# Slot stage of a mixture of experts: marks of the second list two token tiles at a time, inputs turned three slots ahead

## The reference

```python
x = x + attention(layernorm(x), ctx, ...)
y = layernorm(x)
router_weights = softmax(y @ W_router.T + b_router)          # 8 per token
topk_w, topk_idx = top_k(router_weights, 2)                  # the best 2 are kept
x = x + sum over the 2 kept e of topk_w * (y @ W_experts[e].T + b_experts[e])
```

## Time and profile before

| what | value |
|---|---|
| median of 3 runs | 2568.51 us (2566.49 to 2568.64) |
| profiled execution: time | 2569.43 us |
| profiled execution: span | 2567.6 us |
| PE busy | 2446.4 us (95% of the span) |
| DVE busy | 2155.9 us (84%) |
| ACT busy | 1854.7 us (72%) |
| POOL busy | 426.9 us (17%) |

### The profile page before, as it was taken

One profiled execution on the slowest core, in us unless ns is written; L12 is line 12 of the kernel. 1 busy time (PEld: TensorE's weight loads), 2 busy tenths in 40 slices (PEclk: granted clock), 3 DMA queues, 4 the chain that ended last, 5 costly groups with the idle time before them and its releaser, 6 DMA issues. The chain is left out here.

```text
span 2567.6 us, 37487 instructions
## 1 busy us (share of the span) xinstructions
PE 2446.4 (95%) x13675; PEld 1318.7 (51%) x13675; DVE 2155.9 (84%) x1895; ACT 1854.7 (72%) x2174; POOL 426.9 (17%) x522
## 2 busy tenths in 40 slices
PE   8999579999999999999999999999999969879998
PEld 7878324444444444444444444444444438768786
DVE  4368479999999999999999999999999956666565
ACT  3123369999998999999999989999999835513343
POOL 2123200000000000000000000000000024325664
PEclk9999789999999999999999999999999989969999
DMA  7435781111152111124111112311111058624473
GB/s 266 157 137 208 173 213 26 26 29 27 26 124 51 26 30 26 29 56 116 26 30 26 40 33 64 94 26 26 47 26 26 18 170 294 215 84 135 127 235 119
DMA packets 141949, 231.62 MB, mean 90 GB/s; under 512 B 25027, under 2 KB 70595, under 8 KB 141005
## 3 DMA queue, kind: packets, MB, share of 16 engines
q1 hardware_dynamic: 119532, 177.58, 24.2%
q0 software_dynamic: 22240, 51.68, 6.7%
HBM read 155.33 MB, written 91.66 MB: 96 GB/s over the span
## 5 line engine op out<-in xcount | busy, mean ns | idle before, releaser
L1050 ACT ACTIVATE probs<-psum 128x1024 f32<-128x1024 f32 x1600 | 1513.2, 1035 | 137.7 <-PE psum L1204 130.7
L1204 PE MATMUL psum<-q_st,k_st 97*128 97x512 f32 x3200 | 923.0, 419 | 43.3 <-DMA q_st<-shift_scratch 23.8
L1204 PEld LDWEIGHTS psum<-q_st,k_st 97*128 97x128 f32 x3200 | 549.3, 189 | 618.3 <-ACT probs L1050 412.3
L1112 DVE TENSOR_TENSOR even_sums<-even_sums,probs 128x2048 f32<-128x2048 f32 x352 | 806.5, 2291 | 18.3 <-ACT probs L1050 18.3
L1225 PE MATMUL psum<-probs,v_st 128*32 128x512 f32 x6400 | 800.4, 601 | 0.0
L1112 DVE TENSOR_TENSOR odd_sums<-odd_sums,probs 128x2048 f32<-128x2048 f32 x320 | 732.1, 2288 | 1.0
L1225 PEld LDWEIGHTS psum<-probs,v_st 128*32 128x32 f32 x6400 | 152.3, 108 | 353.1 <-issue 273.2
L1922 PE MATMUL psum<-we_hi,wo 128*128 x624 | 218.7, 412 | 5.6 <-issue 5.2
L734 POOL DMA_DIRECT2D sum_scratch<-shared_rows x32 | 18.9, 590 | 1214.8 <-ACT shared_rows L1005 1214.4
L1775 ACT ACTIVATE wo<-psum 128x512 fp32r<-128x512 f32 x78 | 46.5, 596 | 129.3 <-PE psum L1908 129.1
L1922 PEld LDWEIGHTS psum<-we_hi,wo 128*128 128x128 f32 x624 | 119.2, 191 | 31.9 <-issue 6.2
(11 more groups left out here) (214 smaller groups left out, 2242.6 us busy)
## 6 DMA issues: line engine op xcount, KB each, us to landing
q_st<-qh_scratch SPq DMA_DIRECT2D x64, 256.0 KB
k_st<-kh_scratch SPq DMA_DIRECT2D x56, 192.0 KB, 3.9
token_rows<-rows SPq DMA_DIRECT2D x8, 1040.0 KB, 5.2
xn<-in_x SPq DMA_DIRECT2D x16, 512.0 KB, 6.7
qh_scratch<-o_hi SPq DMA_DIRECT2D x8, 1024.0 KB, 4.5
ql_scratch<-o_lo SPq DMA_DIRECT2D x8, 1024.0 KB, 7.8
q_st<-ql_scratch SPq DMA_DIRECT2D x32, 256.0 KB
token_rows<-in_x SPq DMA_DIRECT2D x1, 8192.0 KB, 30.1
```

Of the source, the lines that this page charges most:

```text
L1050: nc.scalar.activation(probs[:, p_slot(it, t), 2 * half:2 * half + 2, :], psum[:, 2 * slot:2 * slot + 2, :], ACT.Exp, scale=SCALE).then_in ...
L1112: nc.vector.tensor_tensor(into[:], a, probs[:, p_slot(it, t)], ALU.add).then_inc(added, 1)
L1204: mm = nc.tensor.matmul(psum[:, 2 * slot + h % 2, :], k_st[:, h, t * P:(t + 1) * P], q_st[:, b, h, :], start=True, stop=True)
```

## The change

The marks of the second list are made for two token tiles at a time, beside 16 slots instead of 8; so `index(1)` moves from s = 9 to s = 17. AHEAD goes from 2 to 3: three turns and three lows stand ahead of slot 0, and turn(s + 3) and low(s + 3) stand behind multiply(s) and finish(s). `x_hi` and `x_lo` have four buffers each (XRING), laid into the same tile `wo`. The order on ScalarE stays normal(s + 1), high(s). GpSimd's code, the six `hold` buffers, the two `xs` buffers and the two banks for transposes stay.

```diff
     G4 = 4
-    NGR = NTL // G4
+    AT_ONCE = (G4, 2)
     HOLD, RES = 6, 3
-    AHEAD = 2
+    AHEAD = 3
+    XRING = 4
...
-        x_hi = [wo[:, b, 0, :].rearrange("p (k n) -> p k n", k=KT) for b in range(2)]
-        x_lo = [wo[:, b, 1, :].rearrange("p (k n) -> p k n", k=KT) for b in range(2)]
+        x_hi = [wo[:, b % 2, b // 2, :].rearrange("p (k n) -> p k n", k=KT) for b in range(XRING)]
+        x_lo = [wo[:, b % 2, 2 + b // 2, :].rearrange("p (k n) -> p k n", k=KT) for b in range(XRING)]
...
+        def marks_before(k, q):
+            return q + k * (NTL // AT_ONCE[0])
+
+        def found_by(m):
+
+            n = NTL // AT_ONCE[0]
+            return (m + 1) * AT_ONCE[0] if m < n else NTL + (m - n + 1) * AT_ONCE[1]
...
                 def high(s):
                     act.wait_ge(xs_turned, s + 1)
-                    if s >= 2:
-                        act.wait_ge(e_mm, s - 1)
-                    act.activation(x_hi[s % 2], ...).then_inc(xh_done, 1)
+                    if s >= XRING:
+                        act.wait_ge(e_mm, s - XRING + 1)
+                    act.activation(x_hi[s % XRING], ...).then_inc(xh_done, 1)
...
                 def mark(k, q):
-                    m = k * NGR + q
+                    m, w = marks_before(k, q), AT_ONCE[k]
                     if m >= 2:
-                        dve.wait_ge(placed, (m - 1) * G4)
-                    b, us = m % 2, slice(q * G4, (q + 1) * G4)
+                        dve.wait_ge(placed, found_by(m - 2))
+                    b, us = m % 2, slice(q * w, (q + 1) * w)
...
                 def low(s):
                     dve.wait_ge(xh_done, s + 1)
+                    if s >= XRING:
+                        dve.wait_ge(e_mm, s - XRING + 1)
...
                     finish(s)
                     if s + AHEAD < NT2:
                         low(s + AHEAD)
-                    if s < NGR:
+                    if s < NTL // AT_ONCE[1]:
                         mark(1, s)
-                    if s == NGR + 1:
+                    if s == NTL // AT_ONCE[1] + 1:
                         index(1)
...
                 def find(k, q):
-                    m = k * NGR + q
+                    m, w = marks_before(k, q), AT_ONCE[k]
                     pe.wait_ge(marked, 2 * (m + 1))
-                    for u in range(G4):
-                        i = q * G4 + u
+                    for u in range(w):
+                        i = q * w + u
...
                     multiply(s, e)
                     if s + AHEAD < NT2:
                         turn(s + AHEAD)
-                    if 1 <= s <= NGR:
+                    if 1 <= s <= NTL // AT_ONCE[1]:
                         find(1, s - 1)
```

More of the change, by code:

```diff
@@ L1772, in high @@
                     act.wait_ge(xs_turned, s + 1)
-                    if s >= 2:
-                        act.wait_ge(e_mm, s - 1)
-                    act.activation(x_hi[s % 2], psum[:, T_BANK + s % 2, :].rearrange("p (k n) -> p k n", k=KT), ACT.Copy).then_inc(xh_done, 1)
+                    if s >= XRING:
+                        act.wait_ge(e_mm, s - XRING + 1)
+                    act.activation(x_hi[s % XRING], psum[:, T_BANK + s % 2, :].rearrange("p (k n) -> p k n", k=KT), ACT.Copy).then_inc(xh_done, 1)
                 normal(0)
[L1778 to L1785, removed]
+                for s in range(NT2):
+                    if s + 1 < NT2:
+                        normal(s + 1)
+                    high(s)
             @block.vector
@@ L1796, in mark @@
                 def mark(k, q):
-                    m = k * NGR + q
+                    m, w = marks_before(k, q), AT_ONCE[k]
                     if m >= 2:
-                        dve.wait_ge(placed, (m - 1) * G4)
-                    b, us = m % 2, slice(q * G4, (q + 1) * G4)
-                    step(dve.tensor_tensor(at_tile[b][:, :, 1, :], lane[:, 0:NS].unsqueeze(1).to_broadcast([P, G4, NS]),
-                                           tile_of[:, us, k:k + 1].to_broadcast([P, G4, NS]), ALU.is_equal))
-                    dve.tensor_tensor(at_tile[b][:, :, 0, :], at_tile[b][:, :, 1, :], token[:, us].unsqueeze(2).to_broadcast([P, G4, NS]), ALU.mult).then_inc(chain, 1)
+                        dve.wait_ge(placed, found_by(m - 2))
+                    b, us = m % 2, slice(q * w, (q + 1) * w)
+                    places, lanes = at_tile[b][:, 0:w], at_lane[b][:, 0:w, :]
+                    step(dve.tensor_tensor(places[:, :, 1, :], lane[:, 0:NS].unsqueeze(1).to_broadcast([P, w, NS]),
+                                           tile_of[:, us, k:k + 1].to_broadcast([P, w, NS]), ALU.is_equal))
+                    dve.tensor_tensor(places[:, :, 0, :], places[:, :, 1, :], token[:, us].unsqueeze(2).to_broadcast([P, w, NS]), ALU.mult).then_inc(chain, 1)
                     c[0] += 1
-                    dve.tensor_tensor(at_lane[b], lane[:].unsqueeze(1).to_broadcast([P, G4, P]),
-                                      lane_of[:, us, k:k + 1].to_broadcast([P, G4, P]), ALU.is_equal).then_inc(marked, 1)
+                    dve.tensor_tensor(lanes, lane[:].unsqueeze(1).to_broadcast([P, w, P]),
+                                      lane_of[:, us, k:k + 1].to_broadcast([P, w, P]), ALU.is_equal).then_inc(marked, 1)
                     dve.wait_ge(chain, c[0])
-                    dve.tensor_tensor(at_tile[b][:, :, 1, :], at_tile[b][:, :, 1, :], mix[:, us, k:k + 1].to_broadcast([P, G4, NS]), ALU.mult).then_inc(marked, 1)
+                    dve.tensor_tensor(places[:, :, 1, :], places[:, :, 1, :], mix[:, us, k:k + 1].to_broadcast([P, w, NS]), ALU.mult).then_inc(marked, 1)
                 def index(k):
@@ L1822, in low @@
                     dve.wait_ge(xh_done, s + 1)
-                    dve.tensor_tensor(x_lo[s % 2], psum[:, T_BANK + s % 2, :].rearrange("p (k n) -> p k n", k=KT),
-                                      x_hi[s % 2].bitcast(F32), ALU.subtract).then_inc(xl_done, 1)
+                    if s >= XRING:
+                        dve.wait_ge(e_mm, s - XRING + 1)
+                    dve.tensor_tensor(x_lo[s % XRING], psum[:, T_BANK + s % 2, :].rearrange("p (k n) -> p k n", k=KT),
+                                      x_hi[s % XRING].bitcast(F32), ALU.subtract).then_inc(xl_done, 1)
                 def finish(s):
@@ L1870, in _ @@
                 step(dve.scalar_tensor_tensor(out=lane_of[:], in0=tile_of[:], scalar=-float(P), in1=pos[:], op0=ALU.mult, op1=ALU.add))
-                for q in range(NGR):
+                for q in range(NTL // AT_ONCE[0]):
                     mark(0, q)
@@ L1921, in multiply @@
                     for t, (k, A, W) in enumerate(terms):
-                        mm = pe.matmul(psum[:, OUT_BANKS[s % 4], :], A[s % 2][:, k, :], W[:, k, ds(e, 1), :].rearrange("p o n -> p (o n)"),
+                        mm = pe.matmul(psum[:, OUT_BANKS[s % 4], :], A[s % XRING][:, k, :], W[:, k, ds(e, 1), :].rearrange("p o n -> p (o n)"),
                                        start=t == 0, stop=t == len(terms) - 1)
```

## The result

The changed kernel takes 2580.93 us (median of 6 runs, 2576.57 to 2582.87), where the kernel before takes 2567.3 beside it (6 runs): 13.6 us more, a ratio of 1.0048 on record with a 95% interval of 1.0036 to 1.006 (the two medians alone give 1.0053). I had forecast slower, by 6 us, with a range up to 2579; it is slower by more than twice that, and above the range. The profiled execution (2582.87, span 2581.1) is the slowest of the six.

What follows compares the result with a forecast made beforehand. From the first expert product on, the chain was taken as TensorE almost alone (busy 95% of the span). Terms 0.0 + 0.0 + 1.94 + 1.9 + 0.4 + 1.8 = +6.0 us gave 2574.5 us, range 2570.5 to 2579.

Steps and rivals of the forecast that it cites:

- the marks at nothing: Find passes on TensorE, four at a time behind 16 slots: net 0.0 us, bounds 0.3 less and 1.2 more.
- low(41) off the far wait: VectorE at the second list's start: low(41) stands before finish(39), so multiply(41) follows multiply(40) and its turn at once.
- the first gap: TensorE's idle time at the second list's start: 5.17 us shrinks to 2.35, winning 2.8 had nothing else been in the way.
- turn(45) held by gather(45): TensorE stands 6.6 us before turn(45), whose rows come late through GpSimd's queue; multiply(43) ends 1.94 us later.
- the clock's loss behind it: Lower clock on turn(45) and multiply(43) after the 6.6 us gap: +1.9 us, bounds 0 and 2.6.
- the change of lists: Start of the second list: stall at turn(45) 1.94 plus clock loss 1.9, +3.8 us.
- turn(54) is ready at 2471.6: Second list in steady state: turn(54)'s slack falls from 3.9 to 0.7 us, enough unless a gather lands late.
- In the first list ... I find no stall.: First list: its gathers of half-rows are shorter, so no stall was found.
- Marks on VectorE ... I take nothing: VectorE's half-width comparisons, 343 to 685 ns each: 0.63 us idle covers the slot's 0.42 shortening; counted as nothing.
- the turns that wait: Second list, two late gathers: turn(52) +0.4 and turn(56) +1.8 us, bounds 0 and 3.5.
- The rule weighed: Skill page's estimate of 3.2 us for gather(45) against 4.68 in the trace: turn(45) 1.5 earlier; the prediction kept the trace.
- Rival C: Slot loop bound by gathers landing near 6.0 us: 0.23 a slot, 7 us in 30 slots, about 2581.5; chance 0.10.

## Why the prediction was wrong

**Right.** Slower; the marks at nothing (measured alone: ratio 0.9999); the transposes' work unchanged and 0.44 given back at the end; low(41) off the far wait, the first gap shrunk to 2.25 (forecast 2.35); turn(45) held by gather(45), 5.99 (6.6), released by normal(45), though the size is near in part by luck: the gather landed 1.3 later than I counted, and multiply(42) ended later too, at the low clock; the clock's loss behind it, 1.65 (1.9); single waits ahead of turns in the second list. At the change of lists +5.0 instead of +3.8: gather(45) landed after 6.0 instead of 4.68, less the smaller clock loss.

**Failed: "turn(54) is ready at 2471.6 ... the slack falls from 3.9 to 0.7. That holds unless a gather lands late."** It looked at one path from gather to TensorE, the turn. There is a second, and I had it before me at the change of lists ("behind normal(45) on ScalarE stands high(44), behind that low(44) and finish(42)") and there took it for one delay. It is there in every slot: gather(s + 4), normal(s + 4), high(s + 3), low(s + 3), finish(s + 1), and gather(s + 4) itself waits for finish(s - 2). With two ahead the same chain spans four slots (12.98 us), with three ahead three (9.74), while its rounds took 10.0 to 11.7 in the chain. The experiments that show it: ScalarE's order alone gives back 6.6 us; and the first list, where no turn was late, loses nothing once that order is turned.

**Failed: "In the first list ... I find no stall."** Same step. No turn waited there, as I had said; VectorE's order makes the loop, and it reaches TensorE through the marks. With it falls the term "Marks on VectorE ... I take nothing": I had let VectorE's 0.63 of idle time cover the shorter slot, but VectorE spends it waiting for high, and the find blocks come late. Both parts are needed: with marks four at a time the first list does not lose (a slot of 4.12 leaves the round room). By the traces that is 2.1 of the 13.6; the medians differ by 4.

**Mis-sized: the turns that wait.** With the loop cut (high ahead of normal) the second list still lost 4.4, and I had 2.2 from two late gathers. The landings range as before (median 4.35 there, up to 5.9). Three turns waited, 0.55, 0.30 and 0.27: half of what I had forecast. But a wait of TensorE costs 0.7 to 0.9 more than it lasts, which makes 3.4 of the three, and the other 1.0 comes from turns that were released just in time and still broke the overlap. I had counted the waits alone.

**The rule weighed.** By the Trainium skill, "DMA: Bandwidth & Descriptors", section "Anatomy of one DMA", such a transfer would take an estimated 3.2 us. Outside the change of lists there would then have been little to wait for. The changed kernel's gathers land in 2.1 to 6.0, median 4.5 (4.4 in the earlier trace rows); the measurement decides against the rule here.

**Rival C** (the slot loop bound by the gathers, 2581.5, chance 0.10) gave the time that came out. That is luck: it asked for a median landing of 5.1 and more, and it stayed at 4.5.

**Left open.** How the second list's 6.4 us divide between the two loops slot by slot: they share finish, gather and normal, and no run cuts the turn's path and keeps the other. Nor was a seventh `hold` buffer tried, which would give both loops one slot more.

## What to carry to other kernels

A deeper look-ahead does not only give slack: it takes a slot from the round of every loop that passes through the engines' fixed orders. Before adding one, write down for each engine what stands ahead of what, follow each buffer's release round to the same instruction of a later slot, and compare the round's time with that many slots; the profile of before has all its parts. And when a stall is removed, look for the next thing that is issued by the same queue: here GpSimd's, which bounded the change of lists with its gathers, and, once these went first, with its scatters.

## What the runs showed of the hardware

Transposes and products that TensorE begins after a wait for their input cost 0.7 to 0.9 us beyond the wait at full clock. In the chain's pieces the turn takes 0.66 instead of 0.44 and the products 3.05 instead of 2.81, with 0.2 to 0.5 of issue between them:

```profile
2509.78 0.66 PE L1916 MATMUL psum<-ident,shared_rows 128*128 128x128 f32 x4 [1.14 <-ACT shared_rows L1777]
2510.64 0.49 PE L1930 MATMUL psum<-we_hi,wo 128*128 x1 [0.21 <-issue]
```

The products keep their own lengths: the first takes 0.49 here and 0.48 behind a turn that did not wait, and the turn alone takes 0.66 from first start to last end instead of 0.60. What is lost is mostly the overlap, 0.24 between turn and products, and the time between them.

Each indirect DMA holds GpSimd for some 1.02 us (1.45 in one of the rows above), and the next begins about 0.30 later at the earliest. With a gather and a scatter in each slot this is 2.6 of 3.25 us, so one more gather in a slot already makes the queue late (4.4 us from gather(45) to gather(46) above).
